# The last expert stage of a four-layer transformer program: final rows made tile by tile and scattered into the output

## What is computed

```
x = x + tanh(g_xattn[l]) * xattn_l(layernorm(x), ...)      # l = 0..3
x = x + tanh(g_ffn[l])   * ffn_l(layernorm(x), ...)
```

```
def _moe_mlp(x, gate_w, gate_b, w1, w2):
    logits = xf @ gate_w + gate_b
    one_hot = one_hot(argmax(logits, axis=-1), E)
    h = gelu(einsum('td,edh->teh', xf, w1), approximate=True)
    y = einsum('teh,ehd->ted', h, w2)
    return einsum('te,ted->td', one_hot, y)

x = x + _msa(_layernorm(x, ln1_w, ln1_b), w_qkv, w_proj)
x = x + _moe_mlp(_layernorm(x, ln2_w, ln2_b), gate_w, gate_b, w1, w2)
return x
```

## Time and profile before

| | us |
|---|---|
| three runs, median (lowest to highest) | 3355.38 (3348.95 to 3356.7) |
| the profiled execution | 3332.66 |
| its span | 3330.8 |
| TensorE busy in the span | 2947.9 (89%) |
| VectorE busy | 1665.7 (50%) |
| GpSimd busy | 1297.0 (39%) |
| ScalarE busy | 1292.8 (39%) |

### The profile page before, as it was taken

The page is one execution under the profiler, slowest core; times in us unless marked ns, Lnnn a source line. Parts: engine busy times, 40 slices in busy tenths (PEclk is TensorE's granted clock), DMA queues, the critical chain, the costliest instruction groups (busy, mean ns, idle before and its releaser), DMA issues. The chain is left out here.

```text
span 3330.8 us, 41163 instructions
## 1 busy us (share of the span) xinstructions
PE 2947.9 (89%) x15872; PEld 1584.3 (48%) x15883; DVE 1665.7 (50%) x3292; ACT 1292.8 (39%) x1784; POOL 1297.0 (39%) x1044
## 2 busy tenths in 40 slices
PE   6889799999999999586889999957888899988897
PEld 3456334434334444244458889833333323322696
DVE  3635455564455455466662112246662877675301
ACT  4432344434344444346521111123433465565232
POOL 3251267565666556610235222213566210000432
PEclk9989899999999999797999999978998999999898
DMA  4000100000000000000016455520001000000465
GB/s 157 11 24 1 37 5 6 10 6 6 6 10 6 5 5 1 26 0 28 1 42 227 176 209 204 190 76 6 1 13 35 1 1 1 1 1 1 142 225 189
DMA packets 58900, 174.10 MB, mean 52 GB/s; under 512 B 9629, under 2 KB 35538, under 8 KB 45908
## 3 DMA queue, kind: packets, MB, share of 16 engines
q0 software_dynamic: 21712, 127.27, 10.6%
q1 hardware_dynamic: 36996, 44.21, 4.1%
HBM read 144.33 MB, written 27.64 MB: 52 GB/s over the span
## 5 line engine op out<-in xcount | busy, mean ns | idle before, releaser
L1506 POOL TENSOR_TENSOR l1x_added<-l1x_added,l1x_probs 128x1024 f32<-128x1024 f32 x224 | 527.4, 2354 | 264.9 <-ACT l1x_probs L1771 199.3
L1868 DVE TENSOR_REDUCE l1x_tops<-l1x_ring 128x1 f32<-128x512 f32 x512 | 326.7, 685 | 203.7 <-PE l1x_ring L1582 203.2
L1120 DVE TENSOR_REDUCE l3a_halves<-l3a_ring 128x1 f32<-128x512 f32 x512 | 324.8, 683 | 98.4 <-PE l3a_ring L965 94.1
L1771 ACT ACTIVATE l1x_probs<-l1x_slots 128x1024 f32<-128x1024 f32 x256 | 262.0, 1024 | 239.7 <-PE l1x_slots L1626 237.9
L1619 PE MATMUL l1x_slots<-l1x_Q,l1x_K 64*128 64x512 f32 x1152 | 311.1, 617 | 7.4 <-ACT l1x_probs L1769 4.8
L1081 ACT ACTIVATE l3a_probs<-l3a_slots 128x1024 f32<-128x1024 f32 x256 | 248.1, 1021 | 159.2 <-PE l3a_slots L985 159.2
L1641 PE MATMUL l1x_pv<-l1x_probs,l1x_V 128*64 128x512 f32 x1152 | 285.0, 611 | 0.0
L985 PE MATMUL l3a_slots<-l3a_Q,l3a_K 32*128 32x512 f32 x1024 | 149.7, 634 | 35.4 <-ACT l3a_probs L1081 34.6
L3396 DVE TENSOR_TENSOR l2f_hh<-l2f_sg,l2f_hid 128x256 f32<-128x256 f32 (+1 forms) x184 | 69.9, 381 | 214.7 <-ACT l2f_sg L3249 214.7
L3249 ACT ACTIVATE l2f_sg<-l2f_hid 128x256 f32<-128x256 f32 (+1 forms) x184 | 64.6, 352 | 281.4 <-PE l2f_hid L3165 279.1
L3165 PE MATMUL l2f_hid<-l2f_xgT,l2f_gate 128*128 128x256 f32 (+1 forms) x736 | 167.7, 351 | 2.3 <-ACT l2f_xgT L3236 1.5
(11 more groups left out here) (705 smaller groups left out, 5177.9 us busy)
## 6 DMA issues: line engine op xcount, KB each, us to landing
l1x_w<-in_l_qkv SPq DMA_DIRECT2D x16, 384.0 KB, 3.1
slots_in<-zeros POOLq DMA_DIRECT2D x1, 4992.0 KB, 24.1
l2f_yg<-rows_out SPq DMA_DIRECT2D x8, 512.0 KB, 6.7
l2f_xg<-slots_in SPq DMA_DIRECT2D x15, 272.0 KB, 3.6
slots_in<-zeros POOLq DMA_DIRECT2D x1, 2944.0 KB, 31.9
x<-in_x SPq DMA_DIRECT2D x4, 512.0 KB, 17.0
l1f_w<-in_l_w SPq DMA_DIRECT2D x2, 1024.0 KB, 7.3
x<-x SPq DMA_DIRECT2D x4, 512.0 KB, 2.9
```

The source lines that it names most:

```text
L1120: nc.vector.tensor_reduce(halves[:, k % 2, col:col + 1], bank_of(banks[e]), AX.X, ALU.max).then_inc(s["bank_done"], 1)
L1506: ins = nc.gpsimd.tensor_tensor(added[h][:], added[h][:], probs[:, n % PROBS, :, :], ALU.add)
L1771: ins = nc.scalar.activation(p, s2[m % 2], ACT.Exp)
L1868: ins = nc.vector.tensor_reduce(tops[:, e * NT + t, h:h + 1], bank, AX.X, ALU.max)
```

## The change

- Rows of `slots_in1` become 2D + 16 = 528 values (`slot_row`): normalised token, "rest", and 16 times the token number. Rows of `slots_in2` stay at 272.
- The rest is g · x + base. ScalarE writes g · x of a chunk behind each `keep_x` (`scale_rest`, four operations), GpSimd adds `base` (four operations) before it waits for the experts of the tiles. The scatters (now of 528 values) wait for these too.
- VectorE makes the final rows of each tile, `y = g * out_ps + rest`, with the rest out of the loaded slot tile; the first tile takes it from `pick_to`, which therefore is loaded with 272 values a row instead of 16.
- GpSimd scatters these rows straight into the output, which has 2944 spare rows behind its 2048; the numbers of spare rows become row + top · 2048. The gathers, the operation over all of x, the sixteen adding operations and the four stores at the end are gone. In l2f they stay.
- Both `moe` stages have three buffers for slot tiles (`AHEAD`). In l3f a load waits until y of the tile three before has been made; in l2f for the same event as before, with one tile more ahead.
- The clear in the first stage zeroes columns 256 to 511 of `slots_in1` too, with one more DMA.

```diff
             for rows, spare in to_clear:
-                pool.dma_start(rows[:, 0:D].rearrange("(n p) d -> p n d", p=P),
-                               c.zeros[:]....broadcast_to([P, rows.shape[0] // P, D])).then_inc(c.cleared, 16)
-                pool.dma_start(rows[:, D:], spare).then_inc(c.cleared, 16)
+                ids = rows.shape[1] - EXTRA
+                for first in range(0, ids, D):
+                    pool.dma_start(rows[:, first:first + D].rearrange("(n p) d -> p n d", p=P),
+                                   c.zeros[:]....broadcast_to([P, rows.shape[0] // P, D])).then_inc(c.cleared, 16)
+                pool.dma_start(rows[:, ids:], spare).then_inc(c.cleared, 16)
...
-            load(PICKED)
-            load(PICKED + 1)
+            for v in range(PICKED, PICKED + AHEAD):
+                load(v)
...
-            for v in range(PICKED, TILES - 2):
-                sp.wait_ge(s["turned"], v + 1)
+            for v in range(PICKED, TILES - AHEAD):
+                sp.wait_ge(s["y_ready" if direct else "turned"], v + 3 if direct else v + 1)
                 sp.wait_ge(s["ids_taken"], v + 1)
-                load(v + 2)
+                load(v + AHEAD)
...
+            if direct:
+                pool.wait_ge(s["base_loaded"], 16)
+                for n in range(NC):
+                    rest = xn[:, n * CT:(n + 1) * CT, D:ID]
+                    pool.wait_ge(s["rest_scaled"], n + 1)
+                    pool.tensor_tensor(rest, rest, base_sb[:, n * CT:(n + 1) * CT, :], ALU.add).then_inc(s["ids_set"], 1)
...
-            pool.wait_ge(c.cleared, 64)
-            pool.wait_ge(s["ids_set"], 1)
+            pool.wait_ge(c.cleared, 80)
+            pool.wait_ge(s["ids_set"], 1 + NC if direct else 1)
...
+            def scale_rest(n):
+                chunk = slice(n * CT, (n + 1) * CT)
+                nc.scalar.activation(xn[:, chunk, D:ID], x[:, chunk, :], ACT.Copy, scale=c.gates[:, gate:gate + 1]).then_inc(s["rest_scaled"], 1)
...
                 keep_x(n)
+                if direct:
+                    scale_rest(n)
...
-                nc.vector.tensor_copy(y[v % 2][:, 0:n, :], out_ps[v % 2][:, 0:n, :]).then_inc(s["y_ready"], 1)
+                if direct:
+                    if v < PICKED:
+                        dve.wait_ge(s["pick_to_loaded"], 16 * PICKED)
+                    rest = pick_to[:, v, 0:n, 0:D] if v < PICKED else xg[v % AHEAD][:, 0:n, D:ID]
+                    nc.vector.scalar_tensor_tensor(y[v % 2][:, 0:n, :], out_ps[v % 2][:, 0:n, :], c.gates[:, gate:gate + 1], rest,
+                                                   ALU.mult, ALU.add).then_inc(s["y_ready"], 1)
...
-            g = c.gates[:, gate:gate + 1]
-            if base is not None:
-
-                dve.wait_ge(s["base_loaded"], 16)
-                step.add(nc.vector.scalar_tensor_tensor(x[:], x[:], g, base_sb[:], ALU.mult, ALU.add))
-            for j in range(top):
+            for j in range(0 if direct else top):
```

More of the change, by code:

```diff
@@ L34 @@
 ROUND = 1.5 * 2.0 ** 23
-ROW = D + 16
+EXTRA = 16
 class Tally:
@@ L94, in slot_units, with slot_row @@
     return (TOK * top + EXPERTS * (P - 1)) // P
+def slot_row(top):
+    return (D if top > 1 else 2 * D) + EXTRA
 def slot_tiles(top):
@@ L371, in _ @@
             for rows, spare in to_clear:
-                pool.dma_start(rows[:, 0:D].rearrange("(n p) d -> p n d", p=P),
-                               c.zeros[:].unsqueeze(1).broadcast_to([P, rows.shape[0] // P, D])).then_inc(c.cleared, 16)
-                pool.dma_start(rows[:, D:], spare).then_inc(c.cleared, 16)
+                ids = rows.shape[1] - EXTRA
+                for first in range(0, ids, D):
+                    pool.dma_start(rows[:, first:first + D].rearrange("(n p) d -> p n d", p=P),
+                                   c.zeros[:].unsqueeze(1).broadcast_to([P, rows.shape[0] // P, D])).then_inc(c.cleared, 16)
+                pool.dma_start(rows[:, ids:], spare).then_inc(c.cleared, 16)
             def norm(n):
@@ L2903, in moe @@
     slots_in, rows_out = io[f"slots_in{top}"], io["rows_out"]
-    PICKED = top
+    PICKED, AHEAD = top, 3
+    direct = x_out is not None
+    assert direct == (base is not None) == (top == 1)
+    ROW = slot_row(top)
+    ID = ROW - EXTRA
     pick_cols = sum(n for _, n in tiles[:PICKED]) * P
@@ L2933, in moe @@
         wb = [{n: sb(f"{n}{i}", [P, w[n].shape[1]]) for n in weight_names} for i in range(2)]
-        xg = [sb(f"xg{i}", [P, ST, ROW]) for i in range(2)]
+        xg = [sb(f"xg{i}", [P, ST, ROW]) for i in range(AHEAD)]
         xgT = [sb(f"xgT{i}", [P, KD, SLOTS]) for i in range(2)]
@@ L2940, in moe @@
         row_no, slot_no = sb("row_no", [P, TT]), sb("slot_no", [P, pick_cols])
-        pick_to = sb("pick_to", [P, PICKED, ST, 16])
+        pick_to = sb("pick_to", [P, PICKED, ST, ROW - D])
         to_row = sb("to_row", [P, TILES, ST], U32)
@@ L2979, in load @@
                 first, n = tiles[v]
-                sp.dma_start(xg[v % 2][:, 0:n, :], tiles_of(slots_in, first * P, n)).then_inc(s[f"xg_loaded{v % 2}"], 16)
+                sp.dma_start(xg[v % AHEAD][:, 0:n, :], tiles_of(slots_in, first * P, n)).then_inc(s[f"xg_loaded{v % AHEAD}"], 16)
             sp.wait_ge(s["scattered0"], 16 * TT)
@@ L3000, in _ @@
                 sp.wait_ge(s[f"y_stored{i}"], 16 * sum(n for v, (_, n) in enumerate(tiles[:-1]) if v % 2 == i))
-            if top > 1:
+            if not direct:
                 collect(0)
             sp.wait_ge(s["last_stored"], 16)
[L3004 to L3009, removed]
+            if not direct:
+                collect(1)
         @block.gpsimd
@@ L3060, in _ @@
                 pool.wait_ge(s["scattered0"], 16 * TT)
-                pool.tensor_scalar(xn[:, :, D:], xn[:, :, D:], float(TOK), None, ALU.add).then_inc(s["ids_moved"], 1)
+                pool.tensor_scalar(xn[:, :, ID:], xn[:, :, ID:], float(TOK), None, ALU.add).then_inc(s["ids_moved"], 1)
                 pool.wait_ge(s["ids_moved"], 1)
@@ L3148, in turn_tile @@
             def turn_tile(v):
-                i = v % 2
-                pe.wait_ge(s[f"xg_loaded{i}"], 16 * ((v - PICKED) // 2 + 1))
+                i = v % AHEAD
+                pe.wait_ge(s[f"xg_loaded{i}"], 16 * ((v - PICKED) // AHEAD + 1))
                 for k in range(KD):
@@ L3428, in _ @@
                     for t in range(n * CT, (n + 1) * CT):
-                        scale = share[:, j, t:t + 1] if top > 1 else g
-                        ins = nc.vector.scalar_tensor_tensor(x[:, t, :], yg[:, t, j, :], scale, x[:, t, :], ALU.mult, ALU.add)
+                        ins = nc.vector.scalar_tensor_tensor(x[:, t, :], yg[:, t, j, :], share[:, j, t:t + 1], x[:, t, :], ALU.mult, ALU.add)
                         if j < top - 1 or t < (n + 1) * CT - 1:
@@ L3484, in numbers @@
         rows = np.arange(slot_units(top) * P, dtype=np.float32).reshape(-1, 1)
-        arrays[f"spare_rows{top}"] = np.repeat(rows + 2 * TOK, ROW - D, 1)
+        arrays[f"spare_rows{top}"] = np.repeat(rows + top * TOK, EXTRA, 1)
         arrays[f"slot_numbers{top}"] = np.concatenate([np.arange(first * P, (first + n) * P, dtype=np.float32) for first, n in slot_tiles(top)[:top]])
@@ L3510 @@
         io[n] = nc.dram_tensor(f"in_{n}", v.shape, mybir.dt.from_np(v.dtype), kind="ExternalInput").ap()
-    io["out"] = nc.dram_tensor("out_0", (TOK, D), F32, kind="ExternalOutput").ap()
+    io["out"] = nc.dram_tensor("out_0", (TOK + slot_units(1) * P, D), F32, kind="ExternalOutput").ap()
     io["x6"] = nc.dram_tensor("x_6", (TOK, D), F32, kind="Internal").ap()
@@ L3514 @@
     r = _run(nc, [feed], core_ids=[0])
-    return r.results[0]["out_0"].reshape(B, S, D)
+    return r.results[0]["out_0"][0:TOK].reshape(B, S, D)
 def weights(io, name):
```

19 lines of the change are left out of this document (10 added, 9 removed).

## The result

The changed kernel takes 3381.11 us in the median of six runs (3377.19 to 3385.71), the kernel before 3355.34 in six; the ratio is 1.0083 with a 95% interval of 1.0073 to 1.0094. It is slower by 25.8 us. A second comparison gave 3379.98 against 3350.18, 1.0087 (1.0064 to 1.0111). The prediction said 3363.7, with a range from 3345 to 3371.

The account below looks back on a forecast made before the run. TensorE was taken to bound the last stage's middle, with the edits at tail, router and program start. −17.7 + 6.5 + 1.0 + 18.5 = +8.3 us on the median of 3355.38 gave 3363.7, range 3345 to 3371.

Parts of the forecast that it names:

- The clear at the start: Start of the program: GpSimd's fifth DMA waits until a whole DMA has landed; costs 18.5 us, from 1.5 to 18.5.
- The tail: After TensorE's last product: one VectorE operation and one scatter leave 4.56 of 22.25 us; saves 17.7 us.
- The router: Start of the last stage: GpSimd's four additions hold up VectorE's comparisons; costs 6.5 us, from 1.2 to 9.4.
- one rival: Start waits for the landing, but no port contention in the router: +3.0 us, 3358.4, chance 0.11.
- The first tile: First slot tile of the last stage: longer rows slow scatter landing and load; costs 1.0 us, from 0.4 to 3.3.
- The steady state: Middle of the last stage: VectorE's longer operation, later-issued loads and added bytes stay covered; costs nothing.

## Why the prediction was wrong

- **The clear at the start** is the step that failed: the length of the wait, in the sum and as an upper bound. That the fifth DMA has to wait, and that the whole program stands behind it, was right. "If room is given back only when a whole DMA has landed, it starts at 31.2, +18.5" took the landing of the first DMA, and made it the end of the range. Measured: the wait ends when all that was given out has landed, 52.3, which is +39.6 on TensorE's start and +37.6 us (the added clear alone) on the time. I had weighed designs, on a guess about what a sender knows that no row showed, instead of bounding the wait by the trace: its profile had the landing of the second clear, 11.16 + 31.9 = 43.1, and with 3 MB more at some 400 GB/s behind it a queue that is empty at about 51. That was the far end to keep. It would have put the sum at +28.
- **The tail** was mis-sized: 9.1 us left, not 4.6, 13.2 saved, not 17.7. The work of the tail was right to a tenth (0.48 for 0.47, 0.78 for 0.77 as the way to the scatter, 2.45 for 2.42). What failed is "From the last landing to the end I put the 0.9 us that lie now behind the last store": now GpSimd is last, and 5.4 us follow. (The 0.9 itself was 1.3: it took the median landing of the four stores, 3.7, where the last one's is 3.3.) The 4.50 us issue was the big VectorE operation's doing, as forecast from the row: without it the issue takes 0.98, and in the seven other traces that keep it 4.49 beside 4.47. What in this issue, which also takes row numbers (`l3f_to_row`), was held up, the rows don't tell; a plain DMA in its place was not tried.
- **The router** was right in mechanism and size: +6.0 for 6.5 (4.5 to 6.2 over all traces), with three comparisons let through, each as long as an addition; the version with VectorE's own operations takes it away. That the two engines get into each other's way at a port, as one rival has it in its name, was not shown; what the rows show is the times, 2.33 to 2.42 us beside additions of 2.34.
- **The first tile** was mis-sized inside its bounds: +2.9 where it shows, nothing where TensorE starts late, for 1.0. The upper bound's reason, the loads queued behind, was wrong; the load takes 7.9 to 8.3 us with them and 8.1 without, where it took 5.1 to 6.7.
- **The steady state** was right: no wait for a slot tile behind the first in any trace, and l2f with three buffers lasts 476.4 us against 476.6.

With the measured sizes: −13.2 + 6.0 + 39.6 and 0 to 2.9, together +32.4 to +35.3 us; measured were +25.8 (interval 24 to 32) and +29.8 (21 to 37), both on chips where the first tile costs nothing, so 32.4 is the sum to compare. Of the rest one thing can be read. The first stage lasted 141.8 us in the first trace of the changed kernel and 135.1 in the second, and 5.1 us of the difference arise in its first 17 us, where some of the same products take twice as long. The first row is of the first trace, the second of the second:

```profile
68.05 3.78 PE L453 MATMUL l0x_slots<-l0x_xT,l0x_wq 128*128 128x512 f32 x4
```

```profile
64.75 1.98 PE L453 MATMUL l0x_slots<-l0x_xT,l0x_wq 128*128 128x512 f32 x4
```

The granted clock is 1.00 in both stretches. The short form shows in two of the five traces in which TensorE starts at 50 us or later (the other is that with 512 added rows, 135.0 us) and in none of the nine in which it starts at 18 to 19 (140.6 to 142.2). So a late start may win some 7 us back in a part of the executions; whether that is so or chance is open.

The chances gave 0.29 to slower by over 0.3%, all of them from other mechanisms, and the range ended 10 us short.

## What to carry to other kernels

Here five of GpSimd's DMAs with 16,256 rows in all went out without a wait, and with 16,384 the last one waited, for 31.3 us, until every earlier one had landed, with all that stands behind it on GpSimd. Where large clears or stores with short rows are queued, add up the rows (or bytes; here 8,816 KB went and 8,944 did not) and not the DMAs, and give what is too much to SyncE's queue, which took 2,944 rows here at no cost (a first stage of 140.8 us, against 140.6 and 141.7 before). GpSimd's additions of 128x1024, placed beside a chain of small VectorE operations, stretched the three of them that ran in between from 0.2 us to 2.3 or 2.4 each; VectorE doing the same work in its waits was cheaper by 5 us in the router. And an end handed to GpSimd cost 4 to 6 us that SyncE's end did not.

## What the runs showed of the hardware that I had not expected

- Where GpSimd's fifth DMA waited, it did not go out as the earlier ones landed one by one: 31.3, 31.6, 37.4 and 38.1 us of wait in four kernels, each ending 0.3 to 0.4 us after the landing of the last DMA given out. With 16,256 rows no wait, with 16,384 the full one.
- The kernels in which GpSimd is the last to end take 5.4 to 7.3 us from the last landing to the end (5.4, 7.0 and 7.3 in three kernels), against 1.3 in before.
- The same kernel, before, took 3350.2 and 3355.3 us in two comparisons and 3330.2 and 3330.3 in two on other chips, 20 to 25 us less. On one of the slower kind, TensorE's products that pick the second tile's tokens in l2f start late by 14 to 15 us in all, in kernels of both kinds, and in three of its four traces so do the first tile's hidden products in l3f, by 4.4 to 5.1 us; on two other chips neither happens. In the stretch of the changed kernel's l2f shown above ScalarE and VectorE wait for TensorE (22.03 us for `l2f_turn`, 28.55 for `l2f_out`) and GpSimd works on; the DMA share in two such stretches is 0.42 and 0.44. Why is open; it was not tried.
